# A two-layer graph network on one Trainium2 core: running counts for the window loops, waits on instructions, own semaphores for chain links

## What is computed

```python
# layer 0 (src, dst with self loops added)
xl, xr = x @ W_l, x @ W_r                      # 4 heads of 32
e = sum(leaky_relu(xl[src] + xr[dst], 0.2) * att)     # one number per edge and head
alpha = softmax of e over the edges of one dst
out = segment_sum(alpha * xl[src], dst) + bias
x = layernorm(x + layernorm(out + x) * gamma + beta)
# layer 1
m = x[src] + edge_attr
h = 2 * x + segment_sum(m, dst)
x = layernorm(x + leaky(h @ W1 + b1, 0.01) @ W2 + b2)
```

## Time and profile before

| | us |
|---|---|
| median of three runs | 6094.19 |
| fastest and slowest of them | 6050.7, 6113.99 |
| the profiled execution | 6089.17 |
| its span, first to last instruction | 6087.3 |
| mean granted TensorE clock in it | 0.76 of full speed |

### The profile page before, as it was taken

How to read it: one execution, slowest core, us unless ns; L and a number is a source line. 1 busy time by engine, 2 the same in 40 slices (tenths; PEclk the granted TensorE clock), 3 DMA queues, 4 the chain that set the end, 5 groups by cost and what they waited for, 6 DMA issues and landing times. The chain is left out here.

```text
span 6087.3 us, 81485 instructions
## 1 busy us (share of the span) xinstructions
PE 3357.9 (55%) x19285; PEld 2766.5 (45%) x19286; DVE 2149.8 (35%) x8265; ACT 1591.1 (26%) x3438; POOL 3004.8 (49%) x3150
## 2 busy tenths in 40 slices
PE   5666655565555555555656645455554545545555
PEld 4444443443433444433434535444544545444445
DVE  4444444444444444444444612222222222222222
ACT  3333333333333333333333401111111111111111
POOL 4444444444444444444444155555555555555554
PEclk7777777777777777777777867777777777777777
DMA  5333323232332322222323243333333333333332
GB/s 170 79 81 84 80 77 77 77 80 73 77 79 75 78 78 74 76 78 75 83 75 82 67 96 93 88 91 88 93 91 89 91 88 91 92 89 92 91 89 78
DMA packets 446518, 518.35 MB, mean 85 GB/s; under 512 B 198373, under 2 KB 346536, under 8 KB 446472
## 3 DMA queue, kind: packets, MB, share of 16 engines
q1 hardware_dynamic: 266390, 268.21, 15.3%
q0 software_dynamic: 100032, 208.20, 14.4%
q10 hardware_dynamic: 80050, 41.37, 2.4%
HBM read 470.16 MB, written 47.29 MB: 85 GB/s over the span
## 5 line engine op out<-in xcount | busy, mean ns | idle before, releaser
L791 POOL DMA_INDIRECT row_ring<-xl_table,src_idx x1531 | 1474.9, 963 | 1864.7 <-DVE wmsg L1285 1329.1
L1672 POOL DMA_INDIRECT row_ring<-x_table,src_idx x1563 | 1492.3, 955 | 1173.7 <-issue 618.9
L1747 PE MATMUL ph<-ident,relu_h 128*128 128x128 f32 x196 | 87.0, 444 | 1242.4 <-DVE relu_h L1917 801.8
L894 PE MATMUL pA<-win,last_node 128*1 128x136 f32 x392 | 97.1, 339 | 1136.5 <-ACT win L1057 1068.1
L1747 PEld LDWEIGHTS ph<-ident,relu_h 128*128 128x128 f32 x196 | 34.0, 173 | 1294.9 <-DVE relu_h L1917 817.8
L894 PEld LDWEIGHTS pA<-win,last_node 128*1 128x1 f32 x392 | 20.5, 80 | 1176.8 <-issue 1173.4
L829 PE MATMUL ph<-node_of,xr_win 128*128 128x512 f32 (+1 forms) x782 | 496.7, 770 | 10.0 <-issue 9.2
L1802 ACT ACTIVATE relu_h<-ph,b 128x128 f32<-128x128 f32 x196 | 72.0, 368 | 1472.1 <-PE ph L1752 1263.6
L855 PE MATMUL pT<-att_heads,relu_h 128*128 128x48 f32 x3126 | 414.2, 273 | 62.0 <-issue 56.4
L872 PE MATMUL pA<-wmsg,edge_of 128*128 128x136 f32 x3126 | 422.0, 290 | 4.0 <-DVE edge_of L1318 2.2
L1273 DVE TENSOR_TENSOR logits<-pT,row_ring 128x32 f32<-128x32 f32 x196 | 39.4, 201 | 1084.5 <-remote 1037.9
(11 more groups left out here) (212 smaller groups left out, 6446.3 us busy)
## 6 DMA issues: line engine op xcount, KB each, us to landing
dst_row<-in_dst SPq DMA_DIRECT2D x195, 513.0 KB
dst_row<-in_edge_attr SPq DMA_DIRECT2D x195, 512.0 KB
row_ring<-x_table,src_idx POOLq DMA_INDIRECT x1563
row_ring<-xl_table,src_idx POOLq DMA_INDIRECT x1531
sums_table<-win ACTq DMA_DIRECT2D x196, 68.0 KB
row_ring<-in_x SPq DMA_DIRECT2D x101, 128.0 KB, 2.4
xr_win<-xr_table SPq DMA_DIRECT2D x196, 64.0 KB
relu_h<-x_table SPq DMA_DIRECT2D x196, 64.0 KB
```

Source lines behind the costliest of these rows:

```text
L791: pool.indirect_dma_start(rows_of_slot[s][:, t, 0:DW], None, xl_table[:, :], bass.IndirectOffsetOnAxis(ap=src_idx[k][:, t:t + 1], axis=0))\
L894: pe.matmul(pick, last_node[:, g.c % U:g.c % U + 1], win[:, :], start=True, stop=True)\
L1672: pool.indirect_dma_start(rows[s][:, t, 0:D], None, x1_table[:, :], bass.IndirectOffsetOnAxis(ap=src_idx[U + s][:, t:t + 1], axis=0))\
L1747: pe.transpose(across_bank, x1_slot[s], ident[:, :]).then_inc(S("x1_across"), 1)
```

## The change

Five edits, in both layers unless said:

1. The counts in `spans` become running counts: on VectorE, once, a shift, a copy, a scan over the 196 groups and two copies. Each engine then compares its own running count of further windows with the group's (`windows_to`), so that the loop's counter isn't set to 1 for each group. The separate registers for the node go too (`span[0]` is counted up in place).
2. TensorE and VectorE in layer 0 load one register for each group from a new table `depths`, instead of two from `spans`: TensorE 10 a turn for 20, VectorE 6 for 12.
3. Waits that stood alone join the instruction behind them, where the loop is passed without a turn: for `dst_taken0` before the edges' one-hot, for `first_made` before `last_node`, for `win_ready` before `pick_last`, in layer 1 two waits of `h_in`. The wait for `shifted_ready` behind `shift` goes.
4. TensorE and ScalarE wait on the count's register itself, without a copy (`count = lambda r: r`). `h_ready` and `relu_ready` become one semaphore for each half, so that no doubled value is needed, and TensorE's wait for `relu_ready` in `sources` goes.
5. VectorE's links get semaphores of their own (`fwd_made`, `carry_kept`, `from_made`, `top_begun`, `top_made`), all waited for at one value a group; the merges' roots share theirs between two uses.

```diff
-def sweep(eng, groups, step, ends=None, turn=U, layer=0, back=1):
+def sweep(eng, groups, step, ends, width, turn=U, layer=0, back=1):
...
-            eng.load(regs, ends[0:1, bass.ds(2 * first if j is None else j * (2 * turn), 2 * n)])
+        eng.load(regs, ends[0:1, bass.ds(width * first if j is None else j * (width * turn), width * n)])
...
+def windows_to(eng, done, upto, body):
+
+    with eng.While(lambda: eng.snap(done) < eng.snap(upto)):
+        body()
...
+                v.memset(ones_f, 1.0)
+                link(v.tensor_scalar(span_counts, span_counts, 7, None, ALU.arith_shift_right))
+                link(v.tensor_copy(further_f, span_counts))
+                link(v.tensor_tensor_scan(upto_f, ones_f, further_f, 0.0, ALU.mult, ALU.add))
+                v.tensor_copy(span_counts, upto_f)
+                v.tensor_copy(depths[:, :], upto_f)
...
                     wait_alone(pe, pe_waits, S(f"gathered0{s}"), (g + U).use(16 * T, 16 * tiles(g) - (16 * T if s < U else 0), RING))
-                    if g.at_least(1):
-                        pe.wait_ge(S("relu_ready"), g.times(2, 0))
...
-                    further_windows(pe, n, span, further)
+                    windows_to(pe, n_hide, span[-1], further)
...
-                    wait_alone(pe, pe_waits, S("win_ready"), count(n_win))
+                    pe.wait_ge(S("win_ready"), count(n_win))
...
-                sweep(pe, groups, step, spans, RING)
+                sweep(pe, groups, step, depths, 1, RING)
...
-                    wait_alone(v, v_waits, S("dst_taken0"), g.times(1, U + 1))
...
-                    further_windows(v, n, span, further)
+                    windows_to(v, n_sum, span[-1], further)
+                    v.wait_ge(S("dst_taken0"), g.times(1, U + 1))
                     one_hot(0).then_inc(S("edge_of_made"), 1)
...
-                    soft.link(v.tensor_tensor(top_n, from_fn, by_head(run, n), ALU.max))
-                    soft.link(v.tensor_tensor(top_n, top_n, from_bn, ALU.max))
+                    v.tensor_tensor(top_n, from_fn, by_head(run, n), ALU.max).then_inc(S("top_begun"), 1)
+                    v.wait_ge(S("top_begun"), g.times(1, 1))
+                    v.tensor_tensor(top_n, top_n, from_bn, ALU.max).then_inc(S("top_made"), 1)
+                    v.wait_ge(S("top_made"), g.times(1, 1))
...
-                    wait_alone(v, v_waits, S("shifted_ready"), g.times(1, 1))
...
-                sweep(v, groups, step, spans)
+                sweep(v, groups, step, depths, 1)
...
-                    wait_alone(v, v_waits, S("x1_across"), k.times(1, 1))
-                    wait_alone(v, v_waits, S("z_made"), k.times(1, 1))
+                    v.wait_ge(S("x1_across"), k.times(1, 1))
+                    v.wait_ge(S("z_made"), k.times(1, 1))
```

More of the change, by code:

```diff
@@ L89, in node_loop @@
     steps(None, range(pairs, pairs + max(lag for _, lag in stages)))
-def sweep(eng, groups, step, ends=None, turn=U, layer=0, back=1):
+def sweep(eng, groups, step, ends, width, turn=U, layer=0, back=1):
     pool = []
     def part(j, first, steps, lo, n):
[L99 to L103, removed]
-            eng.load(regs, ends[0:1, bass.ds(2 * first if j is None else j * (2 * turn), 2 * n)])
+        while len(pool) < width * n:
+            pool.append(eng.alloc_register(f"ends{layer}_{len(pool)}"))
+        regs = pool[0:width * n]
+        eng.load(regs, ends[0:1, bass.ds(width * first if j is None else j * (width * turn), width * n)])
         for c in steps:
-            step(Group(j, c, turn), lambda g: (regs[2 * (g.c - lo)], regs[2 * (g.c - lo) + 1]))
+            step(Group(j, c, turn), lambda g: regs[width * (g.c - lo):width * (g.c - lo) + width])
     loops = (groups - back - (turn - 1)) // turn
@@ L235, in build @@
         spans = sb("spans", [1, 2 * groups], I32)
+        depths = sb("depths", [1, groups], I32)
         starts = sb("starts", [1, groups + EXTRA + 2], I32)
@@ L680, in stats_of, with variances @@
             return ins
-        def variances(v, k0, k1, tag, n):
+        def variances(v, k0, k1, tag, n, own):
             wait_alone(v, v_waits, S(f"{tag}_stats"), n)
@@ L725, in _ @@
             def _(sp):
-                base, n, n_more, home = (sp.alloc_register(r) for r in ("sp_base", "sp_n", "sp_n_more", "sp_home"))
+                n_more, home = (sp.alloc_register(r) for r in ("sp_n_more", "sp_home"))
                 sp.reg_mov(n_more, 0)
@@ L771, in step @@
                         load_sources(sp, g + (RING - 1))
-                sweep(sp, groups, step, spans, RING)
+                sweep(sp, groups, step, spans, 2, RING)
                 last_homes = [sp.alloc_register(f"sp_home{k}") for k in range(LAST)]
@@ L802, in _ @@
             def _(pe):
[L803 to L804 removed]
+                n_hide, n_in, n_sum, n_win = (pe.alloc_register(r) for r in ("pe_n_hide", "pe_n_in", "pe_n_sum", "pe_n_win"))
                 for r in (n_hide, n_in, n_sum, n_win):
                     pe.reg_mov(r, 0)
[L807 removed]
+                count = lambda r: r
                 pe.sem_inc(S("xr_more_used"), 1)
@@ L1155, in _ @@
                 last_homes = act_last[:] = [act.alloc_register(f"act_home{k}") for k in range(LAST)]
-                sweep(act, groups, step, spans)
+                sweep(act, groups, step, spans, 2)
                 act.reg_add(n_out, n_out, 16)
@@ L1163, in _ @@
             def _(v):
-                n, n_hide, n_hide_link, n_sum, n_sum_link = (v.alloc_register(r) for r in (
-                    "v_n", "v_n_hide", "v_n_hide_link", "v_n_sum", "v_n_sum_link"))
-                for r in (n_hide, n_hide_link, n_sum, n_sum_link):
+                n_hide, n_sum = (v.alloc_register(r) for r in ("v_n_hide", "v_n_sum"))
+                for r in (n_hide, n_sum):
                     v.reg_mov(r, 0)
-                count = lambda r: v.snap(r, min_val=1, max_val=1 << 20)
+                count = lambda r: r
                 for s in range(U):
@@ L1862, in _ @@
             def _(v):
-                n, at, n_sum = (v.alloc_register(r) for r in ("v1_n", "v1_at", "v1_n_sum"))
+                n_sum = v.alloc_register("v1_n_sum")
                 v.reg_mov(n_sum, 0)
```

118 lines of the change are left out of this document (61 added, 57 removed).

## The result

| | before | changed |
|---|---|---|
| median of 20 runs, us | 6071.46 | 6106.65 |
| fastest, slowest | 5996.17, 6118.88 | 6086.52, 6116.23 |
| profiled execution | 6089.17 | 6093.74 |

The ratio is 1.0086, 95% interval 1.0064 to 1.0107; by the medians of all executions it is 1.0058, 35 us. So the kernel is slower by 0.6 to 0.9%, where 0.4% faster was forecast (25 us). The time lies outside the forecast's own range (6040 to 6085) and inside the one for 8 in 10 (5985 to 6120); the direction was wrong. Ratios with an interval leave out executions more than 1.5% above a kernel's fastest one, which cuts into the wide scatter of before, so medians of all executions stand beside them where this matters. The scatter itself is a result: the executions of before lie over 123 us, those of the changed kernel over 30.

The account below looks back on a forecast made before the run. An order of waits bounds the kernel, with TensorE's signal held under GpSimd's paired layer 0 gathers. From 6089 us, -13 - 8 - 5 + 1 = -25 gives 6064; own range 6040 to 6085, 8 in 10 5985 to 6120.

Parts of the forecast that it names:

- The limit: Layer 0: GpSimd and the other engines stop for each other; TensorE's signal comes 2 to 3 us after paired gathers.
- hold gone: Rival, layer 0: signal no longer held, GpSimd alone bounds at about 11 us a group; 5180 us, chance 0.08 shared.
- pattern opens: Rival, layer 0: signal precedes the second group's gathers, groups alternate singly at some 14 us; 5590 us, chance 0.08 shared.
- TensorE's registers, -13 us: Layer 0 loop turns behind a restart: ten fewer registers save 0.56 us, wholly on the path, 24 times.
- The joined wait, -8 us: TensorE's wait joined in `pick_last`, and the one dropped in `sources`: between 0 and 20 us over some 90 restarts.
- Runs ahead: Rival: joined `win_ready` wait lets TensorE's sequencer turn its loop and load registers inside the hold; 6038 us, chance 0.12.
- VectorE, 0: VectorE's loops in layer 0: up to 1 us a group gained, hidden behind `distance` at restarts; 0 us.
- locks sooner: Rival, slower: earlier VectorE makes early layer 0 groups pair more often; +54 us, 6118 us, chance 0.15.
- The links, 0: VectorE's links with own semaphores: only spare value computations done behind a running instruction; 0 us.
- Layer 1, 0: Layer 1: VectorE and TensorE lose a counter and two waits, but finish 4.5 us before the hold ends; 0 us.

Follow-up runs that it names:

- e17: Kernel before, with GpSimd waiting before each group's layer 0 gathers until ScalarE kept the previous group's sums; with holds 5498.4 us.
- e18: Changed kernel, with GpSimd waiting before each group's layer 0 gathers until ScalarE kept the previous group's sums; with holds 5396.9 us.
- e9: Kernel before with only VectorE's running counts, loops and joined waits in layer 0; with holds 1.0032 of before, medians 6150.5 for 6132.3 us.
- e7: Kernel before with only the links' own semaphores and the dropped `shifted_ready` wait in layer 0; with holds 1.0069, medians 6116.6 for 6072.0 us.
- e13: Changed kernel with an unused memset of 1200 elements on VectorE before each group's edges' one-hot; with holds 5959.2 us, 0.991 of the changed kernel.
- e16: Changed kernel with 16 more transposes on TensorE behind each group's sums, before `pick_last`'s wait; 6150.2 us, 1.023 of the changed kernel.
- e14: Changed kernel with an unused memset of 2300 elements on VectorE before each group's edges' one-hot; with holds 5443.8 us, 0.905 of the changed kernel.
- e8: Changed kernel, with GpSimd waiting before each group's layer 0 gathers until ScalarE kept the previous group's sums; with holds 5385.6 for 6132.3 us, 0.878.
- e5: Changed kernel, nothing further altered, beside before in a session without holds; 4043.4 us, 0.9805 of before.
- e1: Kernel before, unchanged, profiled again in a session without holds; 4121.4 us.

## Why the prediction was wrong

**The limit.** Two engines stopping for each other, a signal held to 2 or 3 us after the gathers: read rightly from the earlier trace rows. That the hold is no fixed property of the program wasn't to be seen in one profile; the rival "hold gone" had 5180 us and, with "pattern opens", 0.08; in two sessions before took 4121.

**TensorE's registers, -13 us.** The load fell from 1419 to 1141 ns, not to 860. The straight line through two loads doesn't hold: in the changed kernel 2 registers take 729 ns, 10 take 1141 and the last 12 take 872. And the saving didn't reach `weigh`. Behind a restart with loop turn `sources` starts 2.27 us after `win` for 2.79 (medians of 22 and 19), half a microsecond sooner, nearly the 0.56 of the sum; but `targets` ends at 8.02 us for 8.03, and `weigh` comes at 11.36 for 11.38. `targets` itself got slower, with the same matmuls, before and then changed:

```profile
1556.79 3.08 PE L829 MATMUL ph<-node_of,xr_win 128*128 128x512 f32 x4
```

```profile
1580.27 3.62 PE L836 MATMUL ph<-node_of,xr_win 128*128 128x512 f32 x4
```

The granted clock goes back from half to full speed 7.35 us after `win` in before and 7.87 us after it in the changed kernel (medians), so that in the first the last of the four matmuls runs at full speed (0.59 us at 1559.27) and in the second it doesn't (1.06 us at 1582.83). TensorE began its work sooner and did more of it at the lower clock. Why the clock rose later isn't shown. The sum had no term for the clock.

**The joined wait, -8 us.** Its own size was right: `pick_last` follows `win` by 0.34 us for 0.43, `sources` by 0.88 for 0.97. Little of it arrived. Take the bursts of two whose signal came after their end and let the next burst start (75 of 84 before, 89 of 91 changed): restart to `weigh` is 9.95 us for 10.03 on average, the gathers take 20.06 us for 20.36, the signal comes 2.86 us after them for 2.75, and the pair takes 34.90 for 35.18. Over all pairs it is 34.86 for 34.82: the nine other pairs of before, in most of which the signal left in the gap inside the burst, took only 31.8 us. This gap is what an earlier second weighing closes. It was over 0.5 us in 36 of the 75, in 17 of the 89. Where pairs of both kinds begin on like groups (number 1 modulo 4, in the changed kernel), the 26 without the gap take 34.38 us and get their signal 2.90 us after the gathers, the 17 with it 33.27 and 2.12. I had taken the release as a constant; with the pairs that slipped through, it is what took back both savings.

**Runs ahead.** Fell, as the MOVE had suggested: the load still starts 0.8 us after `win` and `sources` 2.23 us after it (1575.88, 1578.11), though the wait is joined. The Trainium skill (Perfetto Trace Analysis, Tensor Engine Instruction) says that a pushed instruction takes its wait along and leaves the sequencer free; here the sequencer's load stayed behind the instruction whose wait was open, in all 22 such restarts.

**VectorE, 0.** This is the step that failed. The edit was sized well: gap gone, 0.5 to 1 us a group, measured as 1.05 and 1.13 us on the second weighing (10.35 to 9.30, 9.28 to 8.15). I asked only where its time would be hidden at a restart, behind `distance`, and not what an earlier `weigh` starts. I asked that in the rival "locks sooner", and got its condition right (the second `weigh` before the end of the first group's 10 us of gathers). But I gave it 0.15 and let it act in the early stretch only, since this profile was locked from 649 us on. It opens again at 3277 us, and the three others with the old VectorE do so up to 2427, 2630 and 3285 us. That its working gives +54 us, as much as lies between the two sets of profiles, is luck: it counts 98 early groups where there are 24 up to 508 us and 33 up to 649, so that 24 x 1.1 = 26 us would have been its most. By the medians +35 us remain. A warning was on the page: three runs of before lay over 63 us, from a kernel of which I had called the steady state locked. It is a weak sign: with the order fixed the executions lie over 13 and 9 us (e17, e18), but those of e9, whose profile has no late single burst, over 96.

**The links, 0.** Same failure, seen alone in e7: nothing on any path that I followed, and 1.0069.

**Layer 1, 0.** 2551 us for 2535 in the two profiles; over all with holds, outside e13 to e16, 2537 to 2568 with the old code and 2535 to 2553 with the new. Some 8 us may be there; it isn't settled.

What stays open: why some sessions have holds, and what holds TensorE's signals. That the order of the groups takes back what the edits save is shown by work added back (e14) and by the order fixed (e17, e18). That either half of VectorE's edits closes late single bursts rests on one or two profiles of each. The exact 35 us are not shown: in one session the medians of before and changed were equal (6016.6 and 6013.7).

## What to carry to other kernels

Where an order of waits is the limit and has two forms, ask of each edit not what time it saves but which form it favours; an engine that gets earlier can queue work that blocks another. Wide scatter of the times can be a sign of it. And fix the order with a wait of its own: here one wait gave 10 to 12% with holds and cost nothing without (0.9810 of before for 0.9805), and only with it did the edits show with holds what they were worth.

## What the runs showed of the hardware

- The same kernel took 4121 to 4123 us in two sessions and 6071 to 6132 us in five others (6017 in a sixth). In the slow kind TensorE's signal for `win`, set 4 us or more after the start of a run of indirect gathers without a pause of 1 us, left before their end in 1 of 339 cases (before, changed, e8, e16); set in the first 4 us it left at once in 53 of 62. Without holds all 192 left within 0.5 us (e5). One chip number stood in a session of either kind, so it isn't the chip alone.
- The granted clock of TensorE over layer 0 was 0.95 in e1, where the engine was busy for 1731 of 1959 us, and 0.75 in the changed kernel with holds, where it was busy for 1865 of 3318.
- Behind a hold of some 15 us the clock came back to full speed 7.35 us after the restart in before and 7.87 us after it in the changed kernel, which began its matmuls 0.5 us sooner (medians of 19 and 22 restarts with loop turn).
- One register load of 12 registers took 872 ns and one of 10 1141 ns in the same kernel.
